# Splitting the next layer's weights in mid-layer, and finishing the output item by item

## The reference

```python
x = x + time_mixing(layernorm(x))                # scan over 512 tokens
r = x                                            # kept for the last residual
x = layernorm(x)
for i in range(6):                               # DIM 128, 16 heads of 64, window 32
    x = attn_layer(x, Wqkv[i], qs[i], ks[i], Wo[i]) + x
    x = ffn_layer(x, g[i], b[i], W1[i], b1[i], W2[i], b2[i]) + x
out = r + x

def attn_layer(x, Wqkv, qs, ks, Wo):
    q, k, v = split(x @ Wqkv, 3)                 # with shifted tokens, 3 x 1024 columns
    q, k = l2norm(q) * qs, l2norm(k) * ks        # per head, then rotary tables
    p = softmax(8 * q @ k.T + mask)              # own and previous window of 32
    return (p @ v) @ Wo
def ffn_layer(x, g, b, W1, b1, W2, b2):
    a, gate = split(layernorm(x) * g + b @ W1 + b1, 2)   # shifted tokens too
    return a * gelu(gate) @ W2 + b2
```

## Time and profile before

| what | value |
| --- | --- |
| median of 3 runs (lowest, highest) | 1795.9 us (1795.12, 1799.96) |
| profiled execution, device time | 1795.17 us |
| its span in the profile | 1793.4 us |
| mean granted TensorE clock | 0.965 of full speed |
| PE busy | 1619.5 us, 90% |
| PEld busy | 1247.0 us, 70% |
| DVE busy | 1467.1 us, 82% |
| ACT busy | 1106.4 us, 62% |
| POOL busy | 992.7 us, 55% |
| POOL, the 36 splits (L134 and L136) | 22.3 us and 46.5 us |
| POOL, the 24 table products (L143) | 17.4 us |
| instruction queue q8 | 257 packets, 4.21 MB |

### The profile page before, as it was taken

How to read it: one execution, slowest core, us unless ns; L and a number is a source line. 1 busy time by engine, 2 the same in 40 slices (tenths; PEclk the granted TensorE clock), 3 DMA queues, 4 the chain that set the end, 5 groups by cost and what they waited for, 6 DMA issues and landing times. The chain is left out here.

```text
span 1793.4 us, 75405 instructions
## 1 busy us (share of the span) xinstructions
PE 1619.5 (90%) x31917; PEld 1247.0 (70%) x32013; DVE 1467.1 (82%) x3193; ACT 1106.4 (62%) x1990; POOL 992.7 (55%) x952
## 2 busy tenths in 40 slices
PE   5369999899999889999989999999999989999985
PEld 2147777677777767777767777767777767777762
DVE  8768888888888888888888888888888788888852
ACT  5236666566666656666656666666666656666652
POOL 2246646665555666555666546676556485565420
PEclk8579999999999999999999999999999999999998
DMA  3011111211101210111111111111101111011101
GB/s 100 26 51 36 39 28 31 77 32 36 50 24 36 61 46 27 47 36 36 56 42 38 47 36 35 52 46 39 47 24 39 59 47 39 24 47 39 36 14 48
DMA packets 40597, 74.95 MB, mean 42 GB/s; under 512 B 8992, under 2 KB 22088, under 8 KB 40264
## 3 DMA queue, kind: packets, MB, share of 16 engines
q1 hardware_dynamic: 40264, 70.11, 13.3%
HBM read 20.08 MB, written 2.10 MB: 12 GB/s over the span
## 5 line engine op out<-in xcount | busy, mean ns | idle before, releaser
L773 POOL TENSOR_TENSOR qk<-qk,qk_sin 128x512 f32<-128x512 f32 x384 | 490.9, 1278 | 217.0 <-DVE qk_sin L847 217.0
L781 POOL TENSOR_TENSOR qk<-qk,rnorm 128x512 f32<-128x512 f32 x384 | 400.4, 1043 | 371.7 <-DVE rnorm L884 371.7
L1024 ACT ACTIVATE squares<-bank 128x512 f32<-128x512 f32 x384 | 228.9, 596 | 168.2 <-DVE qk_sin L847 166.5
L1150 PE MATMUL bank<-w_hi,xs_hi 128*128 128x512 f32 x576 | 290.9, 505 | 14.0 <-ACT squares L1024 7.9
L857 DVE TENSOR_REDUCE norm<-squares 128x8 f32<-128x512 f32 x384 | 258.2, 677 | 30.7 <-ACT squares L1024 28.5
L841 DVE TENSOR_TENSOR qk<-bank,tables 128x512 f32<-128x512 f32 x384 | 261.5, 681 | 6.8 <-PE bank L1152 5.8
L847 DVE TENSOR_TENSOR qk_sin<-bank,tables 128x512 f32<-128x512 f32 x384 | 261.1, 680 | 0.0
L1160 PE MATMUL bank<-ident,qk 128*128 128x128 f32 x1536 | 236.5, 277 | 5.8 <-POOL qk L781 5.1
L1152 PE MATMUL bank<-w_hi,xs_lo 128*128 128x512 f32 x576 | 229.7, 399 | 0.0
L1151 PE MATMUL bank<-w_lo,xs_hi 128*128 128x512 f32 x576 | 228.3, 396 | 0.0
L1160 PEld LDWEIGHTS bank<-ident,qk 128*128 128x128 f32 x1536 | 184.8, 141 | 54.5 <-POOL qk L781 5.9
(11 more groups left out here) (161 smaller groups left out, 2588.1 us busy)
## 6 DMA issues: line engine op xcount, KB each, us to landing
v<-v SPq DMA_DIRECT2D x96, 390.0 KB, 3.5
v<-v SPq DMA_DIRECT2D x72, 130.0 KB, 3.4
w_raw<-in_L_ffn_Wqkv SPq DMA_DIRECT2D x36, 256.0 KB, 3.2
w_o_s<-in_L_ffn_Wo SPq DMA_DIRECT2D x6, 512.0 KB, 5.2
w_s<-in_L_ffn_W SPq DMA_DIRECT2D x6, 341.0 KB, 4.8
mix_x_nat<-in_L_attn_x SPq DMA_DIRECT2D x4, 256.0 KB, 3.7
x_res_scratch<-mix_x_res SPq DMA_DIRECT2D x4, 256.0 KB, 2.7
f_x_res<-x_res_scratch SPq DMA_DIRECT2D x4, 256.0 KB, 3.5
```

Of the source, the lines that this page charges most:

```text
L773: pool.tensor_tensor(qk[:, g % 2, c, :], qk[:, g % 2, c, :], qk_sin[:, c, :], ALU.add).then_inc(added[c], 1)
L781: pool.tensor_tensor(view, view, rnorm[:, g % 2, c * HPC:(c + 1) * HPC].unsqueeze(2) .to_broadcast([P, HPC, DH]), ALU.mult).then_inc(norme ...
L1024: act.activation(squares[:, c % 2, :], bank_of(Q0 + c)[:], ACT.Square).then_inc(squared[c], 1)
L1150: pe.matmul(bank_of(c)[:], l_hi, w_hi[:, cols], start=True, stop=False)
```

## The change

Three things change.

1. `w_hi` and `w_lo` become a ring of eight slots of one chunk; chunk c of layer L lies in slot `(6L + c) % 8`. Two slots are free while a layer runs, so V0 and Q0 of the next layer are split at the end of its steps 8 and 9. Q1 and K0 stay in step 15, and K1 and V1 move to the first step of the next layer. The tables move from the end of step 14 to the end of step 11. The loads follow: chunks V0 and Q0 behind the `move_v` of step 6, Q1 and K0 behind that of step 10, K1 ahead of and V1 behind that of step 15.
2. In the last layer, POOL adds r to the first residual of each item (`add_first_residual`, at t=0), so that `finish_item` gives the output; PE transposes it (`turn_out`, t=2), ACT copies it (`take_out`) and SP stores it. The block of `finish` is gone. r and the output use the two raw buffers.
3. To make room, `xc` and `xn` share a buffer, and `xsq` and `gated` do; two waits on ACT change with them.

```diff
 class SplitWeights:
+    SLOTS = 8
-        self.hi, self.lo = sb("w_hi", [P, 3 * INNER], F32R), sb("w_lo", [P, 3 * INNER], F32R)
+        self.hi, self.lo = sb("w_hi", [P, self.SLOTS, CHUNK], F32R), sb("w_lo", [P, self.SLOTS, CHUNK], F32R)
+    def slot(self, layer, c):
+        return (W_CHUNKS * layer + c) % self.SLOTS
...
+        xc = xn = sb("xc_xn", [P, SEQ])
+        xsq = gated = sb("xsq_gated", [P, SEQ])
+        x_res, o_nat = weights.raw[:, 0, :], weights.raw[:, 1, :].rearrange("p (j c) -> p j c", c=P)
...
+            def load_x_res(m):
+                if not last(m):
+                    return
+                b = m % BATCH
+                need(sp, x1_full, b)
+                sp.wait_ge(raw_used, W_CHUNKS * DEPTH)
+                sp.dma_start(x_res, x_res_dram[:, b, :]).then_inc(x_res_loaded, 16)
+            def store(m):
...
+                sp.wait_ge(out_taken, b + 1)
+                sp.dma_start(out[b].rearrange("(j p) c -> p j c", p=P), o_nat).then_inc(out_stored, 16)
...
                     if t == NBLK - 2:
                         load_w_o(layer)
-                    for c in range(2) if t == NBLK - 2 else range(2, W_CHUNKS):
-                        weights.load(sp, w_qkv, layer, c)
+                    if t == NBLK - 1:
+                        weights.load(sp, w_qkv, layer, 4)
                 move_v(step)
+                if (item + 1) % BATCH == 0 and layer < DEPTH and t == NBLK - 1:
+                    weights.load(sp, w_qkv, layer, 5)
+                if item % BATCH in (1, 2) and layer_of(item) + 1 < DEPTH and t == 2:
+                    for c in range(2):
+                        weights.load(sp, w_qkv, layer_of(item) + 1, 2 * (item % BATCH - 1) + c)
+                if t == 2:
+                    load_x_res(item - 1)
+                    store(item - 2)
                 if item % BATCH == 1 and 1 <= layer_of(item) < DEPTH and t == 2:
                     load_w_1(layer_of(item))
                     load_w_2(layer_of(item))
...
+            def add_first_residual(m):
...
+                pool.wait_ge(x_res_loaded, 16 * (b + 1))
+                pool.wait_ge(xs2_ready, 2 * (m + 1))
+                pool.tensor_tensor(x1[:, m % 2, :], x1[:, m % 2, :], x_res, ALU.add).then_inc(x1_full, 1)
...
+                middle = item % BATCH == 2 and layer + 1 < DEPTH
+                ending = item % BATCH == BATCH - 1 and layer + 1 < DEPTH and t == NBLK - 1
+                opening = item % BATCH == 0 and 0 < layer < DEPTH and t == 0
+                def split_weights(layer, c):
+                    if c < 2:
+                        need(pool, projected[K1 + c], BATCH * NBLK * (layer - 1))
+                    else:
+                        pool.wait_ge(projected[c - 2], BATCH * NBLK * layer)
+                    weights.split(pool, layer, c)
...
                 normalise(step - 1, 3)
                 add(step - 1, 2)
+                if opening:
+                    split_weights(layer, K1)
                 normalise(step - 1, 0)
-                split_weights(V0)
+                if ending:
+                    split_weights(layer + 1, Q1)
                 add(step, 0)
+                if opening:
+                    split_weights(layer, V1)
                 normalise(step - 1, 2)
-                split_weights(Q0)
                 add(step, 1)
+                if ending:
+                    split_weights(layer + 1, K0)
...
                 normalise(step - 1, 1)
-                split_weights(Q1)
-                split_weights(K0)
+                if t == 0:
+                    add_first_residual(item - 2)
                 add(step, 3)
-                split_weights(K1)
-                split_weights(V1)
-                if before_layer and t == NBLK - 2:
-                    weights.make_tables(pool, layer, qk_rows, rot)
+                if middle and t == 3:
+                    weights.make_tables(pool, layer + 1, qk_rows, rot)
+                if middle and t in (0, 1):
+                    split_weights(layer + 1, t)
...
+            def take_out(m):
...
+                act.wait_ge(out_turned, b + 1)
+                need(act, out_stored, 16 * b)
+                act.copy(o_nat.rearrange("p j c -> p (j c)"), bank[5][:]).then_inc(out_taken, 1)
...
+            def turn_out(m):
...
+                pe.wait_ge(x2_done, m + 1)
+                need(pe, shifted[1], NBLK * (m + 2) + 1, BLOCKS)
+                for j in range(NBLK):
+                    mm = pe.transpose(bank[5][:, j * P:(j + 1) * P], batch_slot(m)[:, j * P:(j + 1) * P], ident[:])
+                mm.then_inc(out_turned, 1)
```

More of the change, by code:

```diff
@@ L704, in layer_of, with last @@
             return item // BATCH
+        def last(item):
+            return ITEMS - BATCH <= item < ITEMS
         def batch_slot(item):
@@ L757, in _ @@
                     load_w_2(layer_of(item))
+            sp.wait_ge(out_stored, 16 * BATCH)
         @block.gpsimd
@@ L1121, in _ @@
                 take_probs(step - 2, 1)
+                if t == 2:
+                    take_out(item - 2)
                 if t == 0:
@@ L1343, in _ @@
                     expand(item - 2, 0)
+                if t == 2:
+                    turn_out(item - 2)
                 if t == 3:
```

97 lines of the change are left out of this document (32 added, 65 removed).

## The result

The changed kernel takes 1773.7 us (median of four runs, 1768.05 to 1776.84) against 1795.5 for the kernel before (four runs, 1791.16 to 1799.96): a ratio of 0.9875, with an interval of 0.984 to 0.991. The forecast was 1766 us in a range of 1753 to 1780. The profiled execution is the shortest of the four: 1768.05 us, with a span of 1766.3, 27.1 less than the profiled one of before, where 29.1 were forecast.

What follows compares the result with a forecast made beforehand. The prediction took PE to bound the kernel. Gains of 17.6, 11.7, 4.4 and 8.8 us against costs of 5.5, 5.4, 1.5 and 1.0 made -29.1, from 1795.2 to 1766 us, range 1753 to 1780.

Steps and rivals of the forecast that it cites:

- Step 14: Step 14 of five layers: tables and half of the load burst leave, a gain of 17.6 us, bounds 13 to 23.8.
- Step 15: Step 15 of five layers: four splits leave, two stay ahead of the last normalise, a gain of 11.7 us.
- both delays lie side by side: Step 15: PE's 0.65 us normalise wait and the root's 0.75 us delay overlap, giving 15.55 us per step.
- Step 0: Step 0 behind a layer change: PE's 2.66 us wait and the low clock go, a gain of 4.4 us.
- cover of 0.4 us: Step 0: with K1 and V1 split there, the last normalise ends 0.4 us before PE asks for it.
- POOL late in step 0: Rival, chance 0.11: the cover in step 0 fails and PE waits there, 13 us in all, giving 1779 us.
- Step 11: Step 11 of five layers: the tables delay the root by 1.1 us each, 5.5 us; moved loads add 1.5.
- The moved loads, step 7: Step 7 of layers 1 to 4: a megabyte burst adds 1.8 us in three of four layers, costing 5.4 us.
- The end: After the last residual: 13.6 us shrink to 4.8 with the new closing stage, a gain of 8.8 us.
- Loads without effect: Rival, chance 0.1: loads and gaps are unrelated, so step 14 gains only the tables, giving 1767.6 us.
- All free: Rival, chance 0.12: all moved work costs nothing, only the last 1.0 us cost stays, giving 1753.7 us.
- Full price: Rival, chance 0.07: larger bursts cost 3.3 us in each of nine steps 7 and 11, giving 1789 us.

Runs made afterwards that it cites:

- again: The changed kernel itself, unaltered, run once more beside three others: 1779.5 us, 0.9889 of the kernel before.
- k0_late: `all_moved` with K0's split in step 15 behind the last normalise in place of ahead of it: 1763.0 us, 0.9794 of the kernel before.
- tables_12: The changed kernel with the tables made at the end of step 12 in place of step 11: 1772.4 us, 0.9846 of the kernel before.
- ring_only: The changed kernel with the old closing block in place of the item-by-item closing stage: 1779.6 us, 0.989 of the kernel before.
- all_moved: The changed kernel with tables in step 12, V0/Q0 loads in step 4, Q1/K0 loads in step 12, r's load at t=0: 1761.9 us, 0.9816 of before.
- take_late: `all_moved` with ACT's output copy behind the next item's residual shift (t=3), not at t=2's end: 1762.8 us, 0.9789 of the kernel before.
- split_23: `tables_12` with V0/Q0 loaded in step 4 and split in steps 10 and 11, Q1/K0 loaded in step 12: 1767.2 us, 0.9837 of the kernel before.
- half_block: The changed kernel with 64 transposes ahead of PE's first step: 1767.9 us, 0.9827 of the kernel before.
- small_loads: The changed kernel, but from layer 1 on each chunk load brings 8 of its 512 columns: 1767.0 us, 0.9845 of the kernel before.

## Why the prediction was right, and where it was off

The mechanism and the sign were right, and the profiled sum (-27.1 against -29.1) was near. Two terms were mis-sized and one load was missed; other terms came out better. That the sum is near is in part luck: misses of 9.4 us to one side met 7.3 to the other, 2.2 of these in places that the change doesn't touch, and the profile of `again` is only 15.1 us shorter than that of before. The terms below add up to -14.4 - 13.1 - 5.3 + 6.4 + 4.2 + 2.6 - 5.25 = -24.9 us; the other 2.2 lie in steps that the change doesn't touch and in the 1.1 us by which the first full step starts earlier.

*Step 14: -17.6 forecast, -14.4 measured.* The tables and half of the burst left, as said, and step 46 fell to its floor. But step 30 fell only from 20.57 to 17.74. I had given all steps with a gap 15.4, the price of a gap without a burst. Half a megabyte was still loaded there: the three others with a gap take 15.68 to 15.78. And step 30's clock stayed at 0.90, which is chance: in `again` its gap is as long, 1.75 for 1.78 us, and it takes 16.21 at full clock.

*Step 15: -11.7 forecast, -13.1 measured.* 15.57 in step 47 against the 15.55 of the working, and the wait for the normalise was 0.47 to 0.78 in three layers, none in two, for the 0.65 forecast. `k0_late` shows that the lock alone sets the length: the step "both delays lie side by side" held.

*Step 0: -4.4 forecast, -5.3 measured.* The cover of 0.4 us held: PE waits for no normalise there in any layer, and the wait and the low clock behind the root are gone. POOL late in step 0 did not happen.

*Steps 8 and 9: nothing, as forecast.* The root takes 1.97 us there before and after. Steps 8 take as long as before, steps 9 0.6 us more in sum, no more than steps that the change doesn't touch.

*Step 11: +7.0 forecast (5.5 and 1.5), +6.4 measured.* The root takes 3.07 us in place of 2.0, and step 43 grew by 1.07 from 14.81. `tables_12` takes 5.2 of it back, near the 5.5 of the tables.

*The moved loads, step 7: +5.4 forecast in layers 1 to 4, +4.2 measured.* It is near the full 3.3 us where the gap meets the burst (layers 1 and 2: +2.7 each), and nothing, or less, elsewhere (layer 4: 16.07 to 14.97). I had spread 1.8 over three layers. Right for the sum, wrong for each step.

*Missed: step 7 of layer 5, +2.6.* The closing stage was costed by its instructions on PE, ACT and DVE. Its load of r joins the burst of `w_s`. Without it, or with it moved, the step takes 16.4 to 16.7 us (before, `ring_only`, `all_moved`, `take_late`, `k0_late`); with it, and PE's program as it was, 18.0 to 19.0 in six profiles and 16.97 in `split_23`, so the load is the cause, but its price varies from run to run.

*The end: -8.8 forecast, -5.25 measured.* What follows the last residual shrank by 9.5. The step of the prediction that failed is the silence on what comes before it: the last item's chain grew by 4.1 us, for which the term had nothing. By the windows under `take_late`, 1.0 us of it is the closing stage's own work inside that stretch, four transposes above all, and the other 3 go with the clock, 0.77 for 0.84. ACT's copy, which I suspected first, has no part. The clock there differs between kernels with the same instructions in the stretch (0.81 to 0.59), and in `again` it is 0.70. The gap at 1729.95 is no sufficient reason: `half_block` has none there, and 0.68. Why the clock falls where it does stays open.

*Transposes of the output in steps 90 and 94: +1.0 forecast, nothing measured.* The latter takes 13.88 after 13.86.

*From the profile to the median.* The sum was made in the shortest of four executions. The median lies 5.7 us above it, while before's profile is at its median. `again`, on another chip, has 1778.3 in its profile with the same program, 7 us of the difference in full steps such as the 19.55 above. So of the miss of 7.7 us some 2 are the terms, and 6 are the spread of single executions, in gaps and clock.

*Loads without effect* gave 1767.6, hardly apart from the forecast, so the time could never have told them apart; `small_loads` and the packets under `half_block` did. *All free* is refuted by the tables and by step 7. *Full price* at all nine steps did not come, since a gap was due in the burst only in some.

*The rule against.* The Trainium skill, SBUF — State Buffer, section "Who interferes with whom", says that DMA never contends with a compute engine and that PE never waits on anyone. As a rule on ports no run here contradicts it. As advice that loads may go anywhere it fails: `small_loads` made the steps 7 of layers 1 to 4 5.2 us shorter by bytes alone. That it is the instructions for PE that come late is shown by the packets under `half_block`, by when the gaps end and by the count of 256 between them.

## What to carry to other kernels

Where POOL works at the moment when DVE has a chain of small dependent instructions, count the rest of POOL's instruction for each meeting, and move POOL's work to where it has idle time ahead of the chain. Cost every load that an edit moves or adds by what else is loaded in those microseconds and by whether a block of PE's instructions is due there. And compare the terms of a forecast with the profile step by step: here errors of both signs met in a sum that was near, and the list of steps led to a version at 0.9816 of the kernel before, where the change alone is at 0.9875 to 0.9889.

## What the runs showed of the hardware

PE gets its instructions in blocks of 256, and a gap in `score` ends 1.19 to 1.64 us behind the end of the packet that brings one. Such a gap costs a step 1.5 us without a burst (15.41 against 13.86). In step 39, behind a whole megabyte, it is 2.40 to 3.49 us long. What the step then takes hangs on the clock too, and the gap's length doesn't settle the clock: gaps of 2.41 (`ring_only`) and 3.49 us (`tables_12`) left it at 1.00, with steps of 17.48 and 18.59 us, and gaps of 2.40 to 2.42 (the changed kernel, `again`, `split_23`) went with 0.91 and 18.80 to 19.03. A step 7 without a gap takes 14.8. At the end of the kernel, where PE works in short pieces, the same 196 matmuls take 35.0 us at a granted clock of 0.81 and 42.1 at the 0.59 of `tables_12`.

64 transposes ahead of the first step changed which steps are long, and the full steps of that profile take 7.8 us less than in the first profile of the changed kernel. So an edit that changes the number of PE's instructions can move these gaps, and a difference of some 0.3% between two such kernels may be no more than that. This was tried with one such edit only.
